# A fused attention and LoRA block: one row tile of x split earlier, and TensorE's transposed scores and turned maxima put ahead of the value products

## What is computed

```python
c = x @ W.T + b + 2.0 * (x @ A[idx].T) @ Bm[idx]      # LoRA on the input, R = 16, one slot per batch
q, k, v = c @ w_q, c @ w_k, c @ w_v                    # 32 heads of 32, 8 key/value groups
w = softmax(q @ k.T / sqrt(32)); x = x + (w @ v) @ w_o
y = x @ weight[adapter].T                              # one of 8 matrices of 1024x1024 per batch
gates = softmax(top2(y @ router_w.T))                  # 4 experts, rank 16
x = x + sum_e gates[e] * ((y @ A[e].T) @ B[e].T) * 4
```

## Time and profile before

| | |
|---|---|
| median of 3 runs (lowest, highest) | 1009.52 us (1008.81, 1012.29) |
| profiled execution, whole | 1010.05 us |
| its span from the first to the last instruction | 1008.4 us |
| PE, matmul records | 987.5 us (98%) |
| PEld | 769.9 us (76%) |
| DVE, ACT, POOL | 62%, 45%, 25% |
| granted TensorE clock, mean | 0.998 |

### The profile page before, as it was taken

One profiled execution on the slowest core, in us unless ns is written; L12 is line 12 of the kernel. 1 busy time (PEld: TensorE's weight loads), 2 busy tenths in 40 slices (PEclk: granted clock), 3 DMA queues, 4 the chain that ended last, 5 costly groups with the idle time before them and its releaser, 6 DMA issues.

```text
span 1008.4 us, 16074 instructions
## 1 busy us (share of the span) xinstructions
PE 987.5 (98%) x6228; PEld 769.9 (76%) x6228; DVE 625.9 (62%) x1028; ACT 453.6 (45%) x806; POOL 247.2 (25%) x234
## 2 busy tenths in 40 slices
PE   9999999999999999999999999999999999999996
PEld 6878788777687776877777777786787778778775
DVE  6671822686946778467786688766664654654443
ACT  6121322365744657456665566747441432332221
POOL 1000001033422434223343247645110110110001
PEclk9999999999999999999999999999999999999999
DMA  7030411111411124111142424264999579463432
GB/s 274 0 105 1 136 48 56 43 44 39 128 36 44 50 59 123 44 44 49 44 114 79 110 74 138 86 170 185 276 298 251 165 248 243 143 223 108 164 125 84
DMA packets 72395, 117.33 MB, mean 116 GB/s; under 512 B 7698, under 2 KB 55186, under 8 KB 70816
## 3 DMA queue, kind: packets, MB, share of 16 engines
q1 hardware_dynamic: 62592, 81.70, 28.5%
q0 software_dynamic: 9728, 34.61, 10.0%
HBM read 86.38 MB, written 18.89 MB: 104 GB/s over the span
## 4 chain that ended last, share of the span: by engine, by line
PE 92%; DVE 4%; ACT 1%; POOL 1%; issue 1%; DMA 1%; POOLq 0%; ACTq 0%
PE psP L854 21%; PE psW L1239 17%; PE psF L292 12%; PE psG L1284 8%; PE psO L950 6%; PE psS L926 6%; PE psT L937 5%; PE psX L1580 3%; PE psO L954 3%; DVE nmax L770 2%; PE psF L303 2%; PE psP L876 2%; DVE q_stack L739 1%; PE psP L878 1%; PE psM L961 1%; PE psP L880 1%
## 5 line engine op out<-in xcount | busy, mean ns | idle before, releaser
L630 POOL TENSOR_TENSOR p_sum<-probs 128x512 f32<-128x512 f32 x128 | 168.5, 1317 | 331.7 <-ACT probs L681 331.7
L854 PE MATMUL psP<-x_hl,wq 128*128 128x512 f32 x960 | 237.2, 391 | 0.2 <-DVE v_sb L760 0.2
L770 DVE TENSOR_REDUCE nmax<-psS 128x2 f32<-128x512 f32 x256 | 164.5, 684 | 96.2 <-PE psS L926 91.8
L854 PEld LDWEIGHTS psP<-x_hl,wq 128*128 128x128 f32 x960 | 173.4, 188 | 31.2 <-DVE v_sb L760 0.4
L681 ACT ACTIVATE probs<-psT 128x512 f32<-128x512 f32 x256 | 139.0, 595 | 74.2 <-PE psT L937 73.4
L1239 PE MATMUL psW<-o_split,wq 128*128 128x512 f32 (+1 forms) x600 | 137.5, 383 | 0.0
L1239 PEld LDWEIGHTS psW<-o_split,wq 128*128 128x128 f32 x600 | 108.8, 188 | 21.4
L1269 DVE TENSOR_TENSOR cond_lo<-cond_raw,cond_hi 128x1024 fp32r<-128x1024 f32 x64 | 78.3, 1240 | 54.8 <-ACT cond_hi L1265 54.3
L1265 ACT ACTIVATE cond_hi<-cond_raw 128x1024 fp32r<-128x1024 f32 x64 | 66.5, 1057 | 82.9 <-PE psG L1284 70.2
L739 DVE TENSOR_TENSOR q_stack<-psP,q_stack 32x512 fp32r<-32x512 f32 x128 | 87.8, 686 | 10.2 <-ACT q_stack L646 8.3
L926 PEld LDWEIGHTS psS<-k_stack,q_stack 96*128 96x128 f32 x512 | 79.0, 189 | 16.5 <-DVE q_stack L739 2.1
(11 more groups left out here) (155 smaller groups left out, 1378.4 us busy)
## 6 DMA issues: line engine op xcount, KB each, us to landing
cond_raw<-in_cond POOLq DMA_DIRECT2D x64, 512.0 KB, 4.8
x_raw<-in_xT SPq DMA_DIRECT2D x32, 256.0 KB, 3.2
o_scratch<-o_sb SPq DMA_DIRECT2D x64, 128.0 KB
q_stack<-q_stack SPq DMA_DIRECT2D x31, 256.0 KB, 2.9
q_raw<-in_Wqkv SPq DMA_DIRECT2D x24, 256.0 KB, 3.9
o_pair<-rden_scratch SPq DMA_DIRECT2D x24, 256.0 KB, 9.0
o_pair<-o_scratch SPq DMA_DIRECT2D x6, 1024.0 KB, 13.9
w_raw<-in_W SPq DMA_DIRECT2D x8, 512.0 KB, 7.8
```

The costliest lines, as they stand in the source:

```text
L630: pool.tensor_tensor(p_sum[:, heads], probs[:, 0, heads], probs[:, 1, heads], ALU.add).then_inc(sum_done, 1)
L770: dve.tensor_reduce(nmax[:, n % 2, 2 * hp:2 * hp + 2, qt], psS[:, i % 2].rearrange("p (h k) -> p h k", h=2), AX.X, ALU.max, negate=True).t ...
L854: mm = pe.matmul(out, wq[:, i, w, k * P:(k + 1) * P], x[:, k, part], start=(k == 0 and n_ == 0), stop=False)
```

## The change

It moves instructions and adds none to the arithmetic. In a step, TensorE does the first two transposed scores, then the turned maxima, then the value products. The low part of the fourth x tile (k=3) is made in the first half of step 11 instead of the second, the high part of the fifth in the second half instead of the first. In the very first step DVE takes all four maxima before the low part of q1. In the last steps, the first half of the eighth output tile comes a step earlier, ahead of row 0, and the second half a step later in the attention stage instead of after it; the tiles behind it move up in `first` and `second`. POOL fetches row 6 ahead of its last p_sum (`gpsimd_last`). ScalarE copies g_t before it splits the second row of the next matrix, and DVE adds some output tiles earlier.

```diff
--- before.py
+++ after.py
@@ -339,8 +339,8 @@
 
 
 X_LOAD = {(9, 0): [0, 1], (9, 1): [2], (10, 0): [3, 4], (10, 1): [5], (11, 0): [6, 7]}
-X_HI = {(10, 1): range(4), (11, 0): [4], (12, 0): [5, 6], (12, 1): [7]}
-X_LO = {(11, 0): [0, 1], (11, 1): [3], (12, 1): [5, 6], (13, 0): [7]}
+X_HI = {(10, 1): range(4), (11, 1): [4], (12, 0): [5, 6], (12, 1): [7]}
+X_LO = {(11, 0): [0, 1, 3], (12, 1): [5, 6], (13, 0): [7]}
 X_LO_POOL = {10: 2, 11: 4}
 SEQ = ["v0", "v1", "v2", "v3", "t", "k0", "q0", "q1", "q2", "r0", "r1", "q3", "k1", "q4", "q5", "q6", "q7"]
 NS = len(SEQ)
@@ -626,6 +626,8 @@
                 pool.wait_ge(exp_done, TILES * n + 2 * hp + 2)
                 if n and hp == 0:
                     pool.wait_ge(pv_done, n)
+                if n == N - 1 and hp == 1:
+                    ahead.gpsimd_last(pool)
                 heads = slice(hp * T2, (hp + 1) * T2)
                 pool.tensor_tensor(p_sum[:, heads], probs[:, 0, heads], probs[:, 1, heads], ALU.add).then_inc(sum_done, 1)
             if p + 1 < PAIRS and s + 2 in X_LO_POOL:
@@ -787,7 +789,7 @@
             if more:
                 for k in X_LO.get((s, 0), ()):
                     split_x_lo(dve, p + 1, k, x_lo_done)
-            for unit_ in late(n - 1) if n else [(0, "q1")]:
+            for unit_ in late(n - 1):
                 evacuate(*unit_)
             for unit_ in soon(n, 0):
                 if unit_[1] != "q0":
@@ -797,6 +799,8 @@
                 maxima(n, 2)
                 maxima(n, 3)
                 split_maxima(n)
+            if n == 0:
+                evacuate(0, "q1")
             if p and n < N and s == 6:
                 invert(dve, p - 1)
             if more and s == 8:
@@ -965,13 +969,13 @@
                 scores(n, 0)
                 scores(n, 1)
             run_work(n, 0)
-            if n >= 3:
-                outputs(n - 3)
-            if 1 <= n <= N:
-                turn(n - 1)
             if 2 <= n <= N + 1:
                 scores_t(n - 2, 0)
                 scores_t(n - 2, 1)
+            if 1 <= n <= N:
+                turn(n - 1)
+            if n >= 3:
+                outputs(n - 3)
             if n < N:
                 scores(n, 2)
                 scores(n, 3)
@@ -1189,7 +1193,7 @@
 
     def gpsimd(pool):
         for n in range(B):
-            load_cond(pool, n, range(6, KT) if n == 0 else range(KT))
+            load_cond(pool, n, range(7, KT) if n == 0 else range(KT))
 
         pool.wait_ge(gated_done, B)
         for j in range(YT):
@@ -1315,6 +1319,8 @@
             dve.tensor_tensor(ra_lo[:], ra_raw[:], f(ra_hi[:]), ALU.subtract).then_inc(ra_lo_done, 1)
         if part == 1 and s == 14:
             normalise(dve, 1)
+        if part == 1 and s == 17:
+            residual(dve, KT - 1)
         for r in ROWS_LO.get((s, part), ()):
             cond_row_lo(dve, r)
         if part == 0 and s == 16:
@@ -1331,12 +1337,15 @@
         if s in ROWS_LOAD:
             load_cond(pool, 0, ROWS_LOAD[s])
 
+    def ahead_gpsimd_last(pool):
+        load_cond(pool, 0, [6])
+
     def ahead_tensor(pe, n, part):
         m = FIRST_TILES.get((n - LAST, part))
         if m is not None:
             one_tile(pe, 0, m)
-        if (n - LAST, part) == (17, 0):
-            one_tile(pe, 0, KT - 1, range(4))
+        if (n - LAST, part) in ((16, 0), (17, 0)):
+            one_tile(pe, 0, KT - 1, range(4) if n - LAST == 16 else range(4, KT))
         if (n - LAST, part) == (18, 1):
             pe.wait_ge(o_lo_done, 2)
             one_tile(pe, 1, 0, range(4))
@@ -1375,8 +1384,8 @@
             nc.scalar.activation(fb_stack[:], fb_raw[:], ACT.Copy).then_inc(fb_hi_done, 1)
             copy_g(0)
             cond_row_hi(act, KT)
+            turn_copies(0)
             cond_row_hi(act, KT + 1)
-            turn_copies(0)
 
         def second():
             gates(0)
@@ -1498,8 +1507,8 @@
         def first():
             cond_row_lo(dve, 6)
             dve.memset(beats[:], 0.0).then_inc(chain, 1)
+            residual(dve, KT)
             cond_row_lo(dve, 7)
-            residual(dve, KT - 1)
             before.invert(dve, PAIRS - 1)
             dve.wait_ge(fb_hi_done, 1)
             dve.tensor_tensor(fb_stack[ER:P], fb_raw[ER:P], f(fb_stack[ER:P]), ALU.subtract).then_inc(fb_lo_done, 1)
@@ -1507,10 +1516,10 @@
             cond_row_lo(dve, KT + 1)
 
         def second():
-            residual(dve, KT)
+            residual(dve, KT + 1)
             gates(0)
             for m in range(KT):
-                if m:
+                if m > 1:
                     residual(dve, KT + m)
                 if m < 6:
                     cond_row_lo(dve, KT + m + 2)
@@ -1613,18 +1622,19 @@
         def first():
 
             cond_row(pe, 5)
-            one_tile(pe, 0, KT - 1, range(4, KT))
+            one_tile(pe, 1, 0, range(4, KT))
             cond_row(pe, 6)
             cond_row(pe, 7)
-            one_tile(pe, 1, 0, range(4, KT))
+            one_tile(pe, 1, 1, range(4))
             turn_g(0)
-            one_tile(pe, 1, 1, range(4))
+            one_tile(pe, 1, 1, range(4, KT))
             middle(0)
 
         def second():
             cond_row(pe, KT)
             for m in range(1, KT - 1):
-                one_tile(pe, 1, m, range(4, KT) if m == 1 else range(KT))
+                if m > 1:
+                    one_tile(pe, 1, m)
                 cond_row(pe, KT + m)
             cond_row(pe, KT + 7)
             one_tile(pe, 1, KT - 1, range(4))
@@ -1681,7 +1691,7 @@
             y_two(B - 1, j, last_bank(j), y_done)
 
     ahead.sync, ahead.gpsimd, ahead.scalar, ahead.vector = ahead_sync, ahead_gpsimd, ahead_scalar, ahead_vector
-    ahead.tensor = ahead_tensor
+    ahead.tensor, ahead.gpsimd_last = ahead_tensor, ahead_gpsimd_last
     st.sync, st.gpsimd, st.scalar, st.vector, st.tensor = sync, gpsimd, scalar, vector, tensor
     return st
 
```

## The result

The change makes the kernel slower: 1019.82 us, the median of four runs (1016.61 to 1022.14), against 1009.51 beside it (1008.81 to 1012.29). The ratio is 1.0099, 95% interval 1.0084 to 1.0115. The prediction was 1011.3 us with a range up to 1013.8: wrong, though its largest single term was of the right kind.

What follows compares the result with a forecast made beforehand. TensorE was taken as the bound, matmuls filling 98% of the span. Order +4.5, x tiles -1.2, first step -0.3 and end of attention -1.2 summed to +1.8 us: 1011.3 us median, range 1006.6 to 1013.8.

Steps and rivals of the forecast that it cites:

- order on TensorE, 62 steps: Regular attention steps: psM pays for itself and psS's weight load is exposed, 0.093 us more per step, 5.6 us over 62.
- of these absorbed: Attention steps where TensorE waits for DVE anyhow: 12 of 62 give nothing, leaving 50 x 0.09 = +4.5 us.
- x tiles: Steps 10 to 12 of three pairs: an earlier low part of the fourth tile saves 0.4 us a pair, -1.2 us.
- first step: First attention step: the wait for maxima behind DVE's q1 lows goes, but only 0.3 us is left of it: -0.3 us.
- end of the attention, without the fetch edit: Last steps: moved W_o half -0.5, psT ahead of waiting psO -0.4, earlier g_t copy -0.3 us; together -1.2.
- fetch edit: p_sum less the rows' waits: End of attention: p_sum 1.05 us later, shorter waits for gathered lows of rows 6 and 7; the end's total stays -1.2.
- finish behind row 12: After the attention: later rows keep TensorE's work unchanged, so no term was booked.
- The working of a step: One regular step's stretch from psP to psP in the new order: 2.68 us against 2.60, with psS reading about 0.75.
- Rival A: TensorE's order is neutral: +4.5 falls to about 0, gains stand, -2.7 us, so 1006.8; chance 0.17.
- Rival B: Attention steps absorb little and DVE eats the gains: 5.6 for the order, +4.0 us in all, so 1013.5; chance 0.22.

Runs made afterwards that it cites:

- e1: The kernel before with only TensorE's new order (transposed scores, turned maxima, value products): 1015.69 us, ratio 1.0054.
- e2: The changed kernel with the turned maxima put behind the value products instead of in front: 1018.86 us, ratio 1.0087 to the kernel before.
- e5: The kernel before with only the x tables and the first step's order changed: 1007.29 us, ratio 0.9972.
- e3: The changed kernel without the early fetch of row 6: 1014.14 us, ratio 1.0040 to the kernel before.
- e14: The kernel before with only DVE's batch 3 division by the sums moved later, to m = 5 from 3: 1009.79 us, ratio 1.0003.
- e4: The changed kernel with TensorE's old order and all else kept: 1013.98 us, ratio 1.0020 to the kernel before.
- e6: The changed kernel with TensorE's old order and without the early fetch of row 6: 1008.12 us, ratio 0.9982 to the kernel before.
- e13: The changed kernel with the early fetch of row 6 issued behind the last p_sum instead of ahead: 1017.44 us, ratio 1.0077 to the kernel before.
- e7: e4 with DVE's batch 3 division by the sums moved later, to m = 5 from 3: 1009.85 us, ratio 1.0003 to the kernel before.
- e12: e6 with DVE's batch 3 division by the sums moved later, to m = 5 from 3: 1006.53 us, ratio 0.9973 to the kernel before.
- e15: e12 with the fetch edit added, issued behind the last p_sum: 1009.25 us, ratio 1.0000 to the kernel before.
- e9: The kernel before with only the fetch edit, issued behind the last p_sum: 1012.06 us, ratio 1.0041.
- e10: The changed kernel with DVE's batch 3 division by the sums moved later, to m = 5 from 3: 1018.56 us, ratio 1.0095 to the kernel before.

## Why the prediction was wrong

By its own steps, in us:

| step | predicted | measured |
|---|---|---|
| order on TensorE, 62 steps | +0.093 each | +0.10 each (e1), 0.00 with psM behind psO (e2) |
| of these absorbed | 12, so +4.5 | none; +6.4 with the v_sb waits (e1, from step 0) |
| x tiles | -1.2 | -1.8 (e5) |
| first step | -0.3 | -0.26 (steps 0 and 1 of after) |
| end of the attention, without the fetch edit | -1.2 | -2.05 (e3, step 63 to row 12); -0.6 against e14 |
| fetch edit: p_sum less the rows' waits | 0 (+1.05 - 1.05) | +3.1 (after less e3, step 63 to row 12) |
| finish behind row 12 | 0 | +3.7 in after; +4.5 in e3, +8.6 in e4 |
| sum | +1.8 | +8.8 in the profiled runs (0.3 less from the folding) |

**The working of a step was right.** psP, psT, psM, psO, psS came out at 2.68, the psS group behind psO at 0.75, and e2, which gives psM back its cover, takes exactly this away. Rival A, the order as neutral, is out.

**"I count 12 steps that give nothing" failed.** TensorE's waits for DVE did not absorb a longer step: e1 adds 0.10 in these steps as in all others, and its waits for DVE are as long as in before (4.5 us for 4.4). The likely reason is the program's own chain, in which DVE's maxima follow the psS groups, and ScalarE's exponentials and q copies follow psT and psM, so that an added tenth moves everything by a tenth. Rival B had this right, and e1 is about its 5.6. e2 suggests that an early psM is worth something to ScalarE.

**The row fetch was booked for an exchange that does not exist.** The moved tiles and the g_t copies gave at least about what was booked (1.0 to 2.9 us in e6 for 1.2). The fetch term was "I take 0 for both together", p_sum 1.05 later against shorter waits for rows 6 and 7. Three of its parts failed. Row 6 is not fetched earlier: it is issued 1.29 us behind the exponentials, before 1.30. The price was taken from a_raw, "0.53 for the issue and 0.51 of idle before it", whose index read ran in part under the issue before it; with nothing to cover it the read takes 1.29 us up to the issue, and p_sum is 1.86 late. And the second index read makes row 7 1.4 us later, which the prediction does not mention. What the edit buys is nothing (the wait for the lows is 0.3 with it and without it), what it costs is +3.1 us up to row 12 and 5.7 in the medians (after and e3): 3.3 are there with p_sum on time (e13), 2.4 more come with it late.

**What failed most is the sentence "Later rows keep TensorE's work unchanged".** It is true of the work and wrong of the time. The finish has a second chain, stores, sums' round trip, reciprocals, loads, with the DMA engines at a share above 1.0, and it ends in an instruction of DVE's queue with TensorE's bank releases behind it. Before, that chain ended in time (landed at 741.0, read at 741.59), by a margin of 0.6 us that no row of waits shows. The order alone does not eat it: in e1 TensorE and the chain come later together, and nothing waits. The rest of the change eats it from both sides: the moved tiles make TensorE earlier at row 12 (e6, 4.9 us ahead, with the load landing where before's does), and the fetch edit makes the chain later (e4, whose load lands 6.2 us behind e6's). e4 and e7 show that it is the place in DVE's queue that costs: one moved instruction, and TensorE no longer waits. In e6 and e12 it is the same.

**Not settled.** Why the last o_pair load lands later with the fetch edit is open, as said under e15. So is why many kernels spread over 4 us and more from run to run (e4: 1009.2 to 1016.1, e9: 1009.1 to 1019.9; before itself, in the rounds of e5 and e13, 1008.0 to 1016.6), where e12 spreads over 0.8. A wait of a bank and the clock's fall behind it, there in some runs and not in others, would do for some of it: the 1016.0 of e7 and the two slow runs of e10 (1020.2 and 1020.8) have a mean granted clock of 0.989 and 0.990, where the faster runs of both have 0.995 to 0.998. But e9 has 1016.0 at 0.996, and only one run of each has a trace.

## What to carry to other kernels

A chain that ends just in time leaves no row among the waits. So before work is moved across stages, find for each queue the instruction that waits for a load, see how long the load had landed when it ran, and what stands behind it in that queue. An instruction that is moved up need not run earlier: compare when the load would be issued with when it is issued now, and look for what ran for free under other work, as the index read under p_sum did. And small passes are free only where they stand ahead of a group whose weights must be loaded anyway: look at what each neighbour hides before reordering, and do not count a cost in every turn of a closed loop as absorbed unless a row shows the slack.
